# A twelve-stage latent transformer on one core: set-ups reordered, and variances of the third cross-attention taken in pairs

## The chip, the cores and the metric

The kernel runs on 1 core of one Trainium2 chip. The metric is the device time of one execution in microseconds (us); the number quoted for a kernel is the median of its runs. The engines are PE (TensorE), DVE (VectorE), ACT (ScalarE), POOL (GpSimd) and SP (SyncE, which here only issues DMAs). Each runs its own instructions in order and they meet at semaphores.

## The reference

A latent x of 64 rows by 256 is carried through twelve layers, four rounds of cross-attention, self-attention and feed-forward, each added to x. The context has 6272 rows by 256. The layers that matter here:

- layer 1, self-attention, 16 heads; layer 2, a mixture of experts with a shared one: silu(gate) times up, down, routed experts by a softmax over 8;
- layer 3, cross-attention with queries, keys and values rounded to 127 steps per head; the value rows of the whole context are rounded ahead of it;
- layer 6, the third cross-attention, in 8 groups of heads:

```python
qx = _ln(_fp8_linear_pertensor(ln_out, wqx, ...).reshape(b, s, g, hpg, d), qxln_w, qxln_b)
kvx = jnp.einsum('bsi,oi->bso', cond, w_kv_x)
kx, vx = jnp.split(kvx, 2, axis=-1)
kx = _ln(kx.reshape(b, sc, g, d), kxln_w, kxln_b)
xout = _gqa(qx, kx, vx.reshape(b, sc, g, d)).reshape(b, s, nh * d)
```

Every key of every group is normalised over its own 128 elements, so each of the 8 x 6272 keys needs a variance; a small self-attention (q, k, v over the 64 rows) is joined to it and both are projected;
- layer 10, self-attention with a long convolution, done as a Fourier transform by matrix products; layer 11, a mixture of experts with biases.

## The kernel before

Each layer is a stage with a function for each engine; a stage's set-up is a short serial chain (norm, transposes, projection), and `busy(pe, n, bank)` (L523 to L528) puts n bf16 products on constants into such gaps of PE. Weights come through a ring of four slots in the order of `PIECES`, each load on SP waiting until so many pieces have been used; `x2_kx`, which is wanted last, is loaded first of x2's and keeps its slot longest.

**Values for x1.** DVE rounds 49 tiles of context values (`quantise`, L1706) in pieces of six tiles, two buffers, which ACT narrows to int8 (`narrow_values`, L1714). Pieces 3 and 4 stand in stage 1 before the self-attention, 5 behind it, 6 to 8 in stage 2 (f0) before silu (L892); L917 adds f0's output to x. In x1, DVE scales and rounds the queries (L1935, L1940), PE transposes them, DVE spreads them over a tile (L1947), and the scores follow (L1874).

**x2 (stage 6).** Six weight blocks give queries, keys and values of the 64 rows (`block`, L2132), with turns, heads and normalisation on the other engines. Then come steps: `step(scored, weighed, ahead)` scores group `scored` while it weighs the values of group `weighed`. The first step scores group 0 alone, six steps score group g and weigh g - 1, the seventh as well but with no group ahead, and the last only weighs. The context is cut into 13 chunks (NC), twelve of 512 rows and one of 128. For chunk c PE does, in this order:

```python
for c in range(NC):
    if weighed is not None:
        weigh(weighed, c)                 # L2215, 8 products of 257 columns
    if scored is not None:
        if c + 3 < NC:
            keys(scored, c + 3)           # L2109, 4 products of 512
        if c + 1 < NC:
            variance(scored, c + 1)       # L2188, L2189, 16 of one column
            scores(scored, c + 1)         # L2205, 8 of 128
```

ACT copies the keys (L2597) and squares them (L2604); `low_half` (L2397, DVE) makes the low bf16 half of the squares, which with the high half is averaged by the products of `variance`. `read_var` (L2408, DVE) adds the epsilon, POOL raises to -1/2 (L2733), `scale` (L2420, DVE) multiplies the scores with it, writing over the chunk of S that has just been weighed, `running_max` (L2432) keeps a maximum over chunks. DVE's order in step c is scale(c), read_var(c+1), running_max(c), shift(c+2) of the weighed group (L2455, then exp on ACT, L2665), low_half(c+2). At the group's end `top_of_lanes` (L2438) reduces the maximum over four lanes; PE issues keys 0 and 1 of the group ahead, and then `turn_top` (L2222) transposes it.

**f3 (stage 11)** starts with nine products for the experts' biases (L1327), then the norm (L542) and its transposes (L577); a3 (stage 10) has two places with `busy(pe, 3, 7)` in its middle.

Of the kernel before, what the change touches and what calls it, by code (L numbers as in the profile page):

```python
# [23 lines left out]
T = 64  # L24
D = 256
# [93 lines left out]
def for_query_groups(w):  # L119
# [22 lines left out]
    + [(6, "x2_kx", 2048), (6, "x2_qx0", 2048), (6, "x2_qx1", 2048), (6, "x2_q0", 2048), (6, "x2_q1", 2048), (6, "x2_k", 2048),  # L142
       (6, "x2_v", 2048), (6, "x2_vx", 2048)]
# [198 lines left out]
def perceiver(nc, io, first=0, last=11):  # L342
# [8 lines left out]
    released = [n for _, n, _ in pieces]  # L351
    if "x2_kx" in released:
        released.remove("x2_kx")
        released.insert(released.index("x2_vx"), "x2_kx")
    slot_of, nth_in_slot, release_before = [], [], []
    for n in range(len(pieces)):
        if n < NSLOT:
            slot_of.append(n)
            nth_in_slot.append(1)
            release_before.append(0)  # L360
        else:
            old = piece_no[released[n - NSLOT]]
            slot_of.append(slot_of[old])
            nth_in_slot.append(nth_in_slot[old] + 1)
            release_before.append(n - NSLOT + 1)
# [5 lines left out]
    with ExitStack() as stack:  # L371
        def sb(name, shape, dt=F32):
# [15 lines left out]
            "rounded": (("x1_q_ready", 3, 1), ("x2_in_ready", 6, 2), ("x2_cat_ready", 6, 3)),  # L388
# [10 lines left out]
            "tile_ready": (("x1_tile_ready", 3, 1), ("x2_tile_ready", 6, 2 * GROUPS)),  # L399
# [96 lines left out]
        def W(name):  # L496
            n = piece_no[name]
            if n in late:
                a = sum(pieces[i][2] for i in late[:late.index(n)])
                return keysT[:, :, :].rearrange("p k n -> p (k n)")[:, a:a + pieces[n][2]]  # L500
            return ring[:, slot_of[n], 0:pieces[n][2]]

        def weights_here(eng, name):
# [5 lines left out]
            eng.wait_ge(sem(f"weights_in{slot_of[n]}"), 16 * nth_in_slot[n])  # L509
# [47 lines left out]
        def norm_pool(pool, n):  # L557
            k = norm_no[n]
            if k == 0:
# [5 lines left out]
                     10: (4, 1), 11: (3, 5)}  # L565
# [222 lines left out]
        def self_attention(s, bias):  # L788
# [4 lines left out]
            def dve_(dve):  # L793
                norm_vector(dve, s)
                if s == 1:
                    quantise(dve, 3, 4)
                mha_vector(dve, s)
                if s == 1:
                    quantise(dve, 5)
                residual_vector(dve, s, bank(6, D, T), (sem("projected"), outs.index(s) + 1))  # L800

            def act_(act):
                norm_scalar(act, s)
                if s == 1:
                    narrow_values(act, 3, 4)
                mha_scalar(act, s)
                if s == 1:
                    narrow_values(act, 5)
# [49 lines left out]
        def f0_tensor(pe):  # L858
# [17 lines left out]
            busy(pe, 6, 6)  # L876
# [4 lines left out]
            pe.transpose(ps[:, 3, 0:T], f0_small, C("ident")[0:T, 0:T]).then_inc(sem("f0_hT_psum"), 1)  # L881
            pe.wait_ge(sem("f0_hT"), since("f0_hT", 1))
# [12 lines left out]
        def f0_vector(dve):  # L895
            norm_vector(dve, 2)
            quantise(dve, 6, 7, 8)
# [16 lines left out]
            link(dve, "dve", dve.tensor_reduce(f0_weight, f0_exp, AX, ALU.add))  # L914
            dve.wait_ge(sem("f0_out_psum"), since("f0_out_psum", 1))
# [4 lines left out]
        def f0_scalar(act):  # L920
            norm_scalar(act, 2)
            act.wait_ge(sem("f0_part_psum"), 1)
            act.activation(f0_act, bank(0), ACT.Tanh, scale=0.5).then_inc(sem("f0_tanh"), 1)
            act.wait_ge(sem("f0_hidden_psum"), since("f0_hidden_psum", 1))
            act.activation(f0_small, ps[0:T, 4, 0:128], ACT.Tanh, scale=0.5).then_inc(sem("f0_tanh"), 1)
            narrow_values(act, 6, 7, 8)
# [94 lines left out]
        def f1_vector(dve):  # L1021
# [24 lines left out]
            for n in range(4):  # L1046
# [3 lines left out]
                dve.scalar_tensor_tensor(act, act, f1_pair_gates[:, n:n + 1], u, ALU.mult, ALU.mult).then_inc(sem("f1_hidden"), 1)  # L1050
            dve.wait_ge(sem("f1_lows_psum"), since("f1_lows_psum", 1))
# [4 lines left out]
            if runs(6):  # L1056
                weights_here(dve, "x2_kx")
                x2_key_weights(dve, 0)
# [145 lines left out]
        def a3_tensor(pe):  # L1204
# [22 lines left out]
            busy(pe, 3, 7)  # L1227
# [9 lines left out]
            busy(pe, 3, 7)  # L1237
# [82 lines left out]

        def f3_tensor(pe):
# [1731 lines left out]
```

## Time and profile before

| | |
|---|---|
| runs | 1062.67, 1064.81, 1066.28 us; median 1064.81 |
| profiled execution | 1061.59 us, span 1059.8 us |
| mean granted clock of TensorE | 0.99 of full speed |
| busy share of the span | PE 94%, DVE 68%, ACT 34%, POOL 15% |
| instructions | PE 7822, DVE 1909, ACT 627, POOL 143 |

The profiled execution is the one whose instructions are shown; its time is larger than its span by what lies before the first and behind the last instruction. Busy time is a share of the whole span, over stages with different limits: it doesn't say which engine the others wait for in a given stage. In the timeline a bracket [0.97 <-DMA ...] is the idle time before the instruction and what ended it; instructions without one had no idle time that the trace shows. The two levels of TensorE's clock are 1.2 and 2.4 GHz, shown as 0.50 and 1.00.

### The profile page before, as it was taken

Reading aid. Unit: us, or ns where it says so; the run is one execution under the profiler, and the core shown is the slowest. Engines: PE = TensorE matmul, PEld = TensorE weight load, DVE = VectorE, ACT = ScalarE, POOL = GpSimd, SP = SyncE. Lnnn points to the kernel's source line nnn. Section 1 sums busy time; section 2 is a strip of 40 time slices with the busy share of each in tenths; the row PEclk is TensorE's granted clock in tenths of the full one; section 3 lists DMA queues with packets and bytes.
Section 4 is the critical chain, followed back from the end, with each engine's and each line's share of the span. In section 5 each row is a group of like instructions: output and inputs, shape, how many; then the busy total and the mean of one; then the engine's idle time right before and its main releaser. Section 6 shows DMA issues by size and latency. Waiting matters only on the chain.

```text
span 1059.8 us, 20606 instructions
## 1 busy us (share of the span) xinstructions
PE 994.1 (94%) x7822; PEld 657.2 (62%) x7846; DVE 716.2 (68%) x1909; ACT 358.4 (34%) x627; POOL 156.9 (15%) x143
## 2 busy tenths in 40 slices
PE   6999999998789988899999999999999999988898
PEld 4776677675335544365777777677777777743455
DVE  3777767768779834787676767767676767743343
ACT  2332333334428721443333333333343332301211
POOL 0000000001000010233222323222222323000000
PEclk9999999999999999998999999999999999899999
DMA  7100101002229996860000000000000000232430
GB/s 284 41 22 22 38 20 40 20 5 96 99 62 188 192 313 217 320 241 2 1 1 1 1 0 0 0 0 0 0 0 0 0 1 2 79 140 88 174 159 4
DMA packets 68729, 76.09 MB, mean 72 GB/s; under 512 B 52544, under 2 KB 59456, under 8 KB 64832
## 3 DMA queue, kind: packets, MB, share of 16 engines
q1 hardware_dynamic: 68240, 74.71, 23.1%
q8 instruction: 36, 0.59, 0.2%
q10 hardware_dynamic: 432, 0.62, 0.2%
q14 instruction: 21, 0.17, 0.0%
HBM read 62.41 MB, written 0.07 MB: 59 GB/s over the span
## 4 chain that ended last, share of the span: by engine, by line
PE 73%; DVE 11%; issue 5%; DMA 4%; ACT 3%; POOL 3%; SPq 0%; DVEq 0%; POOLq 0%; PEldq 0%
PE ps L2215 15%; PE ps L2109 13%; PE ps L1480 8%; PE ps L2205 7%; PE ps L1470 4%; PE ps L1491 4%; PE ps L1514 2%; PE ps L1526 2%; POOL x_sum L2733 2%; ACT vals L2016 2%; DMA x_keys<-vals 2%; DVE S L2420 1%; PE ps L528 1%; PE ps L1874 1%; PE ps L2817 1%
## 5 line engine op out<-in xcount | busy, mean ns | idle before, releaser
L2215 PE MATMUL ps<-vals,S 128*128 128x257 f32 x784 | 188.5, 384 | 0.7 <-ACT S L2665 0.7
L2109 PE MATMUL ps<-keysT,row_biases_sb 128*128 128x512 f32 (+1 forms) x416 | 186.3, 573 | 1.0 <-DVE row_biases_sb L2094 0.9
L2733 POOL TENSOR_TENSOR x_sum<-x_max,consts 128x4 f32<-128x4 f32 (+1 forms) x104 | 133.6, 1285 | 322.4 <-DVE x_max L2408 322.4
L2420 DVE SCALAR_TENSOR_TENSOR S<-ps,x_sum,keysT 128x128 f32<-128x128 f32 x392 | 110.9, 344 | 73.3 <-PE ps L2215 64.2
L2215 PEld LDWEIGHTS ps<-vals,S 128*128 128x128 f32 x784 | 143.3, 192 | 19.0 <-issue 1.0
L2665 ACT ACTIVATE S<-S 128x512 f32<-128x512 f32 (+1 forms) x104 | 62.7, 606 | 219.1 <-DVE S L2455 218.5
L2205 PE MATMUL ps<-x_q,x_keys 128*128 128x128 f32 x784 | 114.2, 288 | 0.0
L2109 PEld LDWEIGHTS ps<-keysT,row_biases_sb 128*128 128x128 f32 x416 | 76.6, 192 | 57.7 <-issue 52.6
L2205 PEld LDWEIGHTS ps<-x_q,x_keys 128*128 128x128 f32 x784 | 96.4, 193 | 0.0
L1480 PE MATMUL ps<-ring,S 128*128 128x512 f32 x196 | 92.2, 593 | 0.5 <-DVE ps L1621 0.5
L2597 ACT COPY x_keys<-ps 128x512 f32<-128x512 f32 (+1 forms) x104 | 57.1, 549 | 67.5 <-PE ps L2109 34.3
L1594 ACT ACTIVATE S<-ps 128x2048 f32<-128x2048 f32 (+1 forms) x25 | 46.1, 1843 | 82.3 <-PE ps L1526 76.1
L528 PE MATMUL ps<-consts 128*128 128x512 bf16 x253 | 65.7, 380 | 3.7 <-issue 0.5
L2397 DVE TENSOR_TENSOR sw_key_out<-wide 128x512 bf16<-128x512 f32 (+1 forms) x104 | 67.7, 652 | 0.7 <-ACT wide L2604 0.7
L2455 DVE TENSOR_TENSOR S<-S,xnT 128x512 f32<-128x512 f32 (+1 forms) x104 | 66.7, 654 | 0.3
L2432 DVE TENSOR_TENSOR wide<-wide,S 128x512 f32<-128x512 f32 x96 | 63.3, 659 | 0.3
L2604 ACT ACTIVATE wide<-ps 128x512 f32<-128x512 f32 (+1 forms) x104 | 60.0, 577 | 0.0
L1642 DVE TENSOR_SCALAR S<-ps,mask_sb 128x256 f32<-128x256 f32 x49 | 23.7, 484 | 52.6 <-PE ps L1480 31.1
L1470 PE MATMUL ps<-S,ring 128*128 128x256 f32 (+1 forms) x200 | 50.8, 398 | 8.9 <-DMA S<-ctxT 8.2
L1480 PEld LDWEIGHTS ps<-ring,S 128*128 128x128 f32 x196 | 35.3, 190 | 25.9 <-issue 24.7
L562 POOL TENSOR_TENSOR rstd<-var_eps,consts 64x1 f32<-64x1 f32 x13 | 7.1, 550 | 296.4 <-DVE var_eps L548 260.0
L2408 DVE TENSOR_SCALAR x_max<-ps 128x4 f32<-128x4 f32 (+1 forms) x104 | 16.5, 159 | 48.4 <-PE ps L2189 48.3
(453 smaller groups left out, 1366.1 us busy)
## 6 DMA issues: line engine op xcount, KB each, us to landing
ring<-weights SPq DMA_DIRECT2D x24, 1024.0 KB, 5.9
keysT<-ctxT SPq DMA_DIRECT2D x2, 3136.0 KB, 14.9
vals<-ctxN SPq DMA_DIRECT2D x1, 6272.0 KB, 24.3
S<-ctxT SPq DMA_DIRECT2D x12, 512.0 KB, 4.1
ring<-weights SPq DMA_DIRECT2D x6, 768.0 KB, 7.1
keysT<-weights SPq DMA_DIRECT2D x1, 1792.0 KB, 8.8
keysT<-weights SPq DMA_DIRECT2D x1, 1536.0 KB, 12.0
row_biases_sb<-row_biases SPq DMA_DIRECT2D x1, 1416.0 KB, 12.0
```

Of the source, the lines that this page charges most:

```text
L528: pe.matmul(ps[:, b, :], product[:, 0:128], moving, start=True, stop=True)
L1470: ins = pe.matmul(ps[:, sw_keys_bank, TWO * o:TWO * o + n * TILE], w[:, 256 * k + 128 * o:256 * k + 128 * o + 128], sw_ctxT[ph][:, k, TWO ...
L1480: ins = pe.matmul(bank(sw_vk_bank), sw_ctxT[ph][:, k, a:a + TILE], w[:, 512 + 768 * k:1024 + 768 * k], start=k == 0, stop=k == KT - 1)
L2109: ins = pe.matmul(ps[:, x2_key_bank(g, c), 0:width(c)], x2_wk[:, k, :], ctxT[:, k, span(c)], start=k == 0, stop=k == KT - 1)
L2205: ins = pe.matmul(ps[:, 3 + c % 2, 128 * s:128 * s + 128], x2_keys[:, c % 2, TILE * s:TILE * s + TILE], x2_q[:, :], start=True, stop=True)
L2215: ins = pe.matmul(bank(6, D + 1), S[:, a:a + TILE], ctx_and_ones[:, SUB * c + s, :], start=c == 0 and s == 0, stop=c == NC - 1 and s == su ...
L2397: dve.tensor_tensor(x2_low[c % 2][:, 0:width(c)], x2_dev[:, c % 2, 0:width(c)], high_half(c), ALU.subtract)\
L2420: ins = dve.scalar_tensor_tensor(S[:, a:a + TILE], ps[:, 3 + c % 2, 128 * s:128 * s + 128], x2_inv[:, c % 2, s:s + 1], x2_tile_const, ALU. ...
L2432: ins = dve.tensor_tensor(best, best, S[:, span(c)], ALU.max)
L2455: dve.tensor_tensor(chunk, chunk, spread(x2_top, 1, subs(c)), ALU.subtract).then_inc(sem("x2_shifted"), 1)
L2665: act.activation(chunk, chunk, ACT.Exp, scale=SCALE2).then_inc(sem("x2_exp"), 1)
L2733: pool.tensor_tensor(x2_inv[:, c % 2, 0:n], x2_var[:, c % 2, 0:n], C("neg_half").broadcast_to([128, n]), ALU.pow)\
```

## The change

Set-ups. In stage 1 one piece of values is rounded before the attention and one after it, and in f0 three before silu and one behind the router; the last tile is a piece of its own. x1's scaling by 0.25 is joined to the addition of the bias, POOL scales the bias in stage 2, and rounding, transposes and tile go in two halves. x2's first key weights come by a DMA of their own into `x2_wk`; `x2_kx` moves to the end of x2's pieces, and four loads wait on x2's blocks rather than on the count of used pieces. In x2's set-up turn 3 stands before keys 2 on PE, the heads on ACT before a normalise, two low halves on DVE before a wait. Six of f3's nine bias products stand in a3's two `busy` places.

The loop. Variances are made for chunks (0), (1, 2), (3, 4) to (11, 12) together, on PE in even steps behind keys(c+3); DVE's low_half(c+2) stands in even steps right behind scale(c), in odd ones last; `read_var` and the power handle up to 8 columns at once, 7 times a group for 13. `top_of_lanes` is replaced: the running maximum is folded to 256 and to 128 columns at c = 11 and joined with the last chunk at c = 12.

```diff
-    + [(6, "x2_kx", 2048), (6, "x2_qx0", 2048), (6, "x2_qx1", 2048), (6, "x2_q0", 2048), (6, "x2_q1", 2048), (6, "x2_k", 2048),
-       (6, "x2_v", 2048), (6, "x2_vx", 2048)]
+    + [(6, "x2_qx0", 2048), (6, "x2_qx1", 2048), (6, "x2_q0", 2048), (6, "x2_q1", 2048), (6, "x2_k", 2048),
+       (6, "x2_v", 2048), (6, "x2_kx", 2048), (6, "x2_vx", 2048)]
...
-                     10: (4, 1), 11: (3, 5)}
+                     10: (4, 1), 11: (4, 5)}
...
-                    quantise(dve, 3, 4)
+                    quantise(dve, 3)
                 mha_vector(dve, s)
                 if s == 1:
-                    quantise(dve, 5)
+                    quantise(dve, 4)
...
-            busy(pe, 6, 6)
+            busy(pe, 2, 6)
...
+            busy(pe, 2, 4)
...
-            quantise(dve, 6, 7, 8)
+            quantise(dve, 5, 6, 7)
...
+            quantise(dve, 8)
...
+            narrow_values(act, 5)
             act.wait_ge(sem("f0_part_psum"), 1)
             act.activation(f0_act, bank(0), ACT.Tanh, scale=0.5).then_inc(sem("f0_tanh"), 1)
+            narrow_values(act, 6)
...
+            narrow_values(act, 7, 8)
+        def f0_pool(pool):
+            norm_pool(pool, 2)
+            if runs(3):
+                pool.tensor_scalar(R("q1"), R("q1"), 0.25, None, ALU.mult)
...
+                dve.wait_ge(sem("x2_first_in"), 16)
+                x2_key_weights(dve, 0)
...
-            busy(pe, 3, 7)
+            f3_biases(pe, F3_BIASES[0])
...
-            busy(pe, 3, 7)
+            f3_biases(pe, F3_BIASES[1])
...
+        F3_BIASES = ((0, 1, 4), (2, 3, 5), (6, 7, 8))
+        def f3_biases(pe, places):
+            weights_here(pe, "f3_up0")
+            b1 = W("f3_up0")[:, 2 * F3_UP_WIDTH + KT * 16 + D:]
+            pe.wait_ge(sem("f3_selected"), since("f3_selected", 1))
+            for m in places:
+                pair = F3_ORDER[m]
+                pe.matmul(f3_bank(m), f3_select[:, 128 * pair:128 * pair + 128], b1, start=m % 2 == 0, stop=False, skip_group_check=True)
...
+            f3_biases(pe, F3_BIASES[2])
...
+        value_parts = [(6 * i, 6 * i + 6) for i in range(7)] + [(48, NT), (42, 48)]
...
-            busy(pe, 6, 3)
+            for i in range(2):
+                pe.wait_ge(sem("x1_q_ready"), since("x1_q_ready", i + 1))
+                for j in range(4):
+                    a = 512 * i + 128 * j
+                    ins = pe.transpose(ps[:, X1_TURNED[i], j * T:(j + 1) * T], x1_q_rows[:, a:a + 128], C("ident")[0:T, 0:T])
+                ins.then_inc(sem("x1_qT_psum"), 1)
+            busy(pe, 3, 3)
...
-            link(dve, "dve", dve.tensor_tensor(x1_q, bank(0, D, T), R("q1"), ALU.add))
-            link(dve, "dve", dve.tensor_scalar(x1_q, x1_q, 0.25, None, ALU.mult))
+            link(dve, "dve", dve.scalar_tensor_tensor(x1_q, bank(0, D, T), 0.25, R("q1"), ALU.mult, ALU.add))
...
-            dve.tensor_scalar(x1_q_rows.rearrange("p (j r d) -> p j r d", j=PAIRS, r=4), spread(cut(x1_q, PAIRS, 32), 2, 4), MAGIC, MAGIC,
-                              ALU.add, ALU.subtract).then_inc(sem("x1_q_ready"), 1)
+            for i in range(2):
+                pairs = slice(4 * i, 4 * i + 4)
+                dve.tensor_scalar(x1_q_rows.rearrange("p (j r d) -> p j r d", j=PAIRS, r=4)[:, pairs], spread(cut(x1_q, PAIRS, 32)[:, pairs], 2, 4),
+                                  MAGIC, MAGIC, ALU.add, ALU.subtract).then_inc(sem("x1_q_ready"), 1)
+            x1_tile_of(dve, 0)
...
-            dve.wait_ge(sem("x1_qT_psum"), 1)
-            dve.tensor_tensor(x1_queries.rearrange("p (j h t) -> p j h t", j=PAIRS, h=2), spread(cut(bank(1), PAIRS, T), 2, 2),
-                              spread(spread(C("two_heads"), 1, PAIRS), 3, T), ALU.mult).then_inc(sem("x1_tile_ready"), 1)
+            x1_tile_of(dve, 1)
...
+        x2_behind_block = {"x2_k": 0, "x2_v": 1, "x2_kx": 2, "x2_vx": 3} if runs(5) and runs(6) else {}
+        X2_TOGETHER = [(0,)] + [(c, c + 1) for c in range(1, NC, 2)]
+        X2_READS = len(X2_TOGETHER)
+        x2_read_of = lambda c: (c + 1) // 2
...
-            def variance(g, c):
-                pe.wait_ge(sem("x2_square_low"), g * NC + (c + 1))
-                if c >= 1 or not (isinstance(g, int) and g == 0):
-                    pe.wait_ge(sem("x2_var_read"), g * NC + c)
-                for s in range(subs(c)):
-                    a = SUB * (c % 2) + s
-                    tile_of = slice(TILE * s, TILE * s + TILE)
-                    pe.matmul(ps[:, 7, a:a + 1], high_half(c)[:, tile_of], x2_mean, start=True, stop=False)
-                    ins = pe.matmul(ps[:, 7, a:a + 1], x2_low[c % 2][:, tile_of], x2_mean, start=False, stop=True)
-                ins.then_inc(sem("x2_keys_var"), 1)
+            def variance(g, r):
+                chunks = X2_TOGETHER[r]
+                pe.wait_ge(sem("x2_square_low"), g * NC + (chunks[-1] + 1))
+                if r >= 1 or not (isinstance(g, int) and g == 0):
+                    pe.wait_ge(sem("x2_var_read"), g * X2_READS + r)
+                for c in chunks:
+                    for s in range(subs(c)):
+                        a = SUB * (c % 2) + s
+                        tile_of = slice(TILE * s, TILE * s + TILE)
+                        pe.matmul(ps[:, 7, a:a + 1], high_half(c)[:, tile_of], x2_mean, start=True, stop=False)
+                        ins = pe.matmul(ps[:, 7, a:a + 1], x2_low[c % 2][:, tile_of], x2_mean, start=False, stop=True)
+                    ins.then_inc(sem("x2_keys_var"), 1)
...
                         if c + 3 < NC:
                             keys(scored, c + 3)
+                        if c % 2 == 0 and c + 2 < NC:
+                            variance(scored, c // 2 + 1)
                         if c + 1 < NC:
-                            variance(scored, c + 1)
                             scores(scored, c + 1)
...
-            def read_var(g, c):
-                dve.wait_ge(sem("x2_keys_var"), g * NC + (c + 1))
-                if c >= 2:
-                    dve.wait_ge(sem("x2_inverse"), g * NC + (c - 1))
-                elif c == 0 and not (isinstance(g, int) and g == 0):
-                    dve.wait_ge(sem("x2_inverse"), g * NC)
-                a, n = SUB * (c % 2), subs(c)
-                dve.tensor_scalar(x2_var[:, c % 2, 0:n], ps[:, 7, a:a + n], LN_EPS, None, ALU.add).then_inc(sem("x2_var_read"), 1)
+            def read_var(g, r):
+                dve.wait_ge(sem("x2_keys_var"), g * NC + (X2_TOGETHER[r][-1] + 1))
+                if r >= 1 or not (isinstance(g, int) and g == 0):
+                    dve.wait_ge(sem("x2_inverse"), g * X2_READS + r)
+                n = SUB if r == 0 else 2 * SUB
+                dve.tensor_scalar(x2_max[:, 0:n], ps[:, 7, 0:n], LN_EPS, None, ALU.add).then_inc(sem("x2_var_read"), 1)
...
+                if c == NC - 1:
+                    dve.wait_ge(sem("x2_running"), g * X2_RUNS + X2_RUNS)
+                    dve.tensor_tensor(x2_lanes_top, x2_running[:, 0:128], S[:, span(c)], ALU.max).then_inc(sem("x2_max"), 1)
+                    return
...
-            def top_of_lanes(g):
-                dve.wait_ge(sem("x2_running"), g * NC + NC)
-                dve.tensor_reduce(x2_lanes_top, x2_running.rearrange("p (s r) -> p r s", s=SUB), AX, ALU.max).then_inc(sem("x2_max"), 1)
+            def fold_running(g):
+                for i, n in enumerate((256, 128)):
+                    dve.wait_ge(sem("x2_running"), g * X2_RUNS + (NC - 1 + i))
+                    best = x2_running[:, 0:n]
+                    dve.tensor_tensor(best, best, x2_running[:, n:2 * n], ALU.max).then_inc(sem("x2_running"), 1)
...
                         scale(scored, c, weighed)
-                    if scored is not None and c + 1 < NC:
-                        read_var(scored, c + 1)
+                    if scored is not None and c % 2 == 0 and c + 2 < NC:
+                        low_half(scored, c + 2)
                     if scored is not None:
                         running_max(scored, c)
+                    if scored is not None and c == NC - 2:
+                        fold_running(scored)
                     if weighed is not None and c >= 1 and c + 2 < NC:
                         shift(weighed, c + 2)
-                    if scored is not None and c + 2 < NC:
+                    if scored is not None and c % 2 == 0 and c + 2 < NC:
+                        read_var(scored, c // 2 + 1)
+                    if scored is not None and c % 2 == 1 and c + 2 < NC:
                         low_half(scored, c + 2)
...
+            def inverse(g, r):
+                pool.wait_ge(sem("x2_var_read"), g * X2_READS + (r + 1))
+                if r >= 1 or not (isinstance(g, int) and g == 0):
+                    pool.wait_ge(sem("x2_scores"), since("x2_scores", g * NC + X2_TOGETHER[r][0]))
+                n = SUB if r == 0 else 2 * SUB
+                pool.tensor_tensor(x2_sum[:, 0:n], x2_max[:, 0:n], C("neg_half").broadcast_to([128, n]), ALU.pow)\
                     .then_inc(sem("x2_inverse"), 1)
...
+                if name == "f1_experts3" and runs(6):
+                    first = piece_from["x2_kx"]
+                    sp.dma_start(x2_wk, cut(io["weights"][:, first:first + KT * 1024], KT, 1024)[:, :, 0:GD]).then_inc(sem("x2_first_in"), 16)
...
+                if pieces[n][1] in x2_behind_block:
+                    sp.wait_ge(sem("x2_block_psum"), x2_behind_block[pieces[n][1]] + 1)
+                else:
+                    sp.wait_ge(weights_used, n - NSLOT + 1)
```

## Rows read from the trace of the kernel before

**Rows 1.** Windows: stretch, us; busy PE, PEld, DVE, ACT, POOL; clock, DMA, GB/s.

```profile
431.60:439.00 7.40, 4.86 (x24) 1.48 (x20) 6.22 (x35) 1.81 (x5) 3.08 (x3) 1.00 0.88 302
...
483.40:490.20 6.80, 6.53 (x22) 3.88 (x20) 6.07 (x19) 0.00 (x0) 2.44 (x2) 0.50 0.00 0
...
609.08:667.66 58.58, 58.28 (x355) 42.46 (x355) 41.68 (x115) 20.76 (x42) 16.61 (x13) 1.00 0.00 0
...
903.20:910.00 6.80, 6.29 (x19) 4.71 (x19) 5.41 (x12) 3.79 (x8) 0.00 (x0) 0.50 0.37 117
```

**Rows 2.** Timeline, PE, an even chunk: start, us, engine, line.

```profile
642.78 1.88 PE L2109 MATMUL ps<-keysT,row_biases_sb 128*128 128x512 f32 x4
...
644.50 0.17 PE L2188 MATMUL ps<-sw_value_part,wide 128*128 128x1 bf16 x1
...
644.70 1.14 PE L2205 MATMUL ps<-x_q,x_keys 128*128 128x128 f32 x8
```

**Rows 3.** Timeline, DVE, the same chunk.

```profile
642.98 1.13 DVE L2420 SCALAR_TENSOR_TENSOR S<-ps,x_sum,keysT 128x128 f32<-128x128 f32 x4 [0.77 <-PE ps L2215]
...
646.17 0.68 DVE L2397 TENSOR_TENSOR sw_key_out<-wide 128x512 bf16<-128x512 f32 x1
```

**Rows 4.** Timeline, PE, the end of a group.

```profile
660.05 0.17 PE L2188 MATMUL ps<-sw_value_part,wide 128*128 128x1 bf16 x1
...
663.77 3.60 PE L2109 MATMUL ps<-keysT,row_biases_sb 128*128 128x512 f32 x8
...
667.66 0.33 PE L2222 MATMUL ps<-consts,attendedT 128*128 128x128 f32 x1 [0.30 <-DVE attendedT L2438]
```

**Rows 5.** Timeline, DVE, the same end.

```profile
660.25 1.13 DVE L2420 SCALAR_TENSOR_TENSOR S<-ps,x_sum,keysT 128x128 f32<-128x128 f32 x4 [0.31 <-PE ps L2215]
...
661.30 0.15 DVE L2408 TENSOR_SCALAR x_max<-ps 128x4 f32<-128x4 f32 x1
...
662.23 0.28 DVE L2397 TENSOR_TENSOR sw_key_out<-wide 128x128 bf16<-128x128 f32 x1
...
666.58 1.03 DVE L2438 TENSOR_REDUCE attendedT<-wide 128x128 f32<-128x512 f32 x1
```

**Rows 6.** Instructions of one line, POOL's power: shortest, median, longest in ns.

```profile
L2733 POOL TENSOR_TENSOR x_sum<-x_max,consts x104: 911/1317/1447, 449.6 to 899.1; 128x4 f32<-128x4 f32 x96, 128x1 f32<-128x1 f32 x8
```

**Rows 7.** Timeline, PE, the first step of x2.

```profile
483.17 0.18 PE L2188 MATMUL ps<-sw_value_part,wide 128*128 128x1 bf16 x1 [1.47 <-DVE sw_key_out L2397]
```

**Rows 8.** Timeline, stage 1.

```profile
263.85 3.96 DVE L1706 TENSOR_TENSOR wide<-vals,S 128x1536 int16<-128x1536 f32 x2
...
264.65 1.94 PE L673 MATMUL ps<-ring,xnT 128*64 128x512 f32 x8 [0.45 <-ACT xnT L582]
...
267.73 0.68 DVE L727 TENSOR_TENSOR S<-ps,row_biases_sb 128x512 f32<-128x512 f32 x1
```

**Rows 9.** Timeline, stage 2.

```profile
287.60 0.43 DVE L1706 TENSOR_TENSOR wide<-vals,S 128x256 int16<-128x256 f32 x1 [3.51 <-ACT vals L1714]
...
293.42 0.87 DVE L917 TENSOR_TENSOR x_sb<-x_sb,ps 64x256 f32<-64x256 f32 x2 [0.70 <-PE ps L886]
```

**Rows 10.** Timeline, stage 3.

```profile
299.08 0.28 DVE L1935 TENSOR_SCALAR sw_key_out<-sw_key_out 64x256 f32<-64x256 f32 x1
...
303.61 1.98 PE L1874 MATMUL ps<-keysT,x_probsT 32*128 32x512 f32 x10
```

**Rows 11.** Timeline, set-up of x2.

```profile
436.13 1.94 PE L2132 MATMUL ps<-ring,S 128*64 128x512 f32 x8 [2.19 <-DMA ring<-weights]
```

**Rows 12.** DMA issues of one window, SP: first and last issue, and the landing.

```profile
L2936 SPq DMA_DIRECT2D ring<-weights x1: 328/328/328, 420.5 to 420.5; - x1
...
DMA to landing us min/median/max: 9.6/9.6/9.6
```

**Rows 13.** Timeline, stages 10 and 11.

```profile
1038.43 0.41 DVE L542 TENSOR_SCALAR xn<-x_sb,moments,rstd 64x256 f32<-64x256 f32 x1 [0.66 <-POOL rstd L562]
...
1040.29 0.33 PE L577 MATMUL ps<-consts,xn 64*128 64x64 f32 x2
```

More of the change, by code:

```diff
@@ L350, in perceiver @@
     piece_no = {n: k for k, (_, n, _) in enumerate(pieces)}
[L351 to L365, printed above, removed]
     piece_from, at = {}, 0
@@ L500, in W @@
                 return keysT[:, :, :].rearrange("p k n -> p (k n)")[:, a:a + pieces[n][2]]
-            return ring[:, slot_of[n], 0:pieces[n][2]]
+            return ring[:, n % NSLOT, 0:pieces[n][2]]
         def weights_here(eng, name):
@@ L1323, in f3_tensor @@
             w = W("f3_up0")[:, 2 * F3_UP_WIDTH:]
-            b2, b1 = w[0:NE, KT * 16:KT * 16 + D], w[:, KT * 16 + D:KT * 16 + D + FF]
-            pe.wait_ge(sem("f3_selected"), since("f3_selected", 1))
-            for m, pair in enumerate(F3_ORDER):
-                pe.matmul(f3_bank(m), f3_select[:, 128 * pair:128 * pair + 128], b1, start=m % 2 == 0, stop=False, skip_group_check=True)
+            b2 = w[0:NE, KT * 16:KT * 16 + D]
+            f3_biases(pe, F3_BIASES[2])
             norm_tensor(pe, 11)
@@ L1711, in narrow_values @@
             for part in parts:
-                a, b = 6 * part, min(6 * part + 6, NT)
+                a, b = value_parts[part]
                 act.wait_ge(sem("values_rounded"), part + 1)
@@ L1928, in x1_tensor, with x1_tile_of @@
             out_tensor(pe, 3, attended, w[:, 512:1024], "x1")
+        def x1_tile_of(dve, i):
+            dve.wait_ge(sem("x1_qT_psum"), i + 1)
+            out = x1_queries[:, 512 * i:512 * i + 512].rearrange("p (j h t) -> p j h t", j=4, h=2)
+            dve.tensor_tensor(out, spread(cut(ps[:, X1_TURNED[i], 0:4 * T], 4, T), 2, 2), spread(spread(C("two_heads"), 1, 4), 3, T), ALU.mult)\
+               .then_inc(sem("x1_tile_ready"), 1)
         def x1_vector(dve):
@@ L2088, in x2_key_weights @@
                 dve.wait_ge(sem("x2_keys_psum"), before * NC + NC)
-            of_group = cut(W("x2_kx"), KT, 1024)[:, :, ds(g * GD, GD)]
+            of_group = x2_wk if isinstance(g, int) and g == 0 else cut(W("x2_kx"), KT, 1024)[:, :, ds(g * GD, GD)]
             dve.tensor_reduce(x2_wk_mean, of_group, AX, ALU.add).then_inc(sem("x2_wk_sum"), 1)
@@ L2705, in x2_scalar @@
             take_heads(0)
+            normalise(2)
             take_heads(1)
-            normalise(2)
             copy_const(0)
+            take_heads(2)
             copy_const(1)
-            take_heads(2)
             take_values()
@@ L2739, in x2_pool @@
                     .then_inc(sem("x2_block_inverse"), 1)
-            for c in range(NC):
-                inverse(0, c)
+            for r in range(X2_READS):
+                inverse(0, r)
             with pool.Fori(1, GROUPS) as g:
-                for c in range(NC):
-                    inverse(g, c)
+                for r in range(X2_READS):
+                    inverse(g, r)
         STAGES[6] = (x2_tensor, x2_vector, x2_scalar, x2_pool)
```

53 lines of the change are left out of this document (19 added, 34 removed).

## The prediction

> **What bounds the kernel now.** The profiled execution has a span of 1059.8 us and took 1061.59 us, so 1.8 us lie around the span. By the page's first part PE is busy in 94% of it, VectorE (DVE) in 68%, GpSimd (POOL) in 15%: a faster DVE or POOL pays only where PE waits for it. Then I read the windows, stage by stage: one group step of the third cross-attention (x2) lasts 58.58 us, with PE busy 58.28 of them at clock 1.00 and DVE busy 41.68 [rows 1]. Seven such steps fill 410 us. There the change touches what PE never waits for, so the question is whether the new order makes it wait. The timeline of a chunk [rows 2, 3] and of a group's end [rows 4, 5] answers that; the set-ups are read from their own waits [rows 8 to 13].
>
> **Set-ups and ends, part by part.**
>
> *a1's first piece (stage 1).* The product that L727 reads ends at 264.65 + 1.94 = 266.59, but L727 starts at 267.73, with no wait of its own: two quantise instructions (3.96 us together, from 263.85) stand in front [rows 8]. With one of them behind the attention L727 starts about 0.09 after the product, as after any product: gain 267.73 − 266.68 = 1.05. The piece that moved lies beside the attention's last products on PE, for which DVE has nothing else; uncovered it would cost its 1.98.
>
> *f0 (stage 2).* The last small quantise waited 3.51 us for ScalarE's (ACT) narrowing and stood ahead of silu; it goes [rows 9]. Then the other end limits: the big quantise moved behind the router (1.75 us, the second half of a 1.98-us one without its narrow) stands before L917, which was at 293.42 and can be at about 291.7. Gain 1.7. If the quantise were hidden, PE's order would allow 2.45. The removed dummy products are only as long as the wait they filled.
>
> *x1 (stage 3).* One multiply goes (0.28 busy, 0.32 with its link; the scaling of q1 moves to POOL, which could cost no more than one power-sized instruction, 0.9, if it were not), and rounding, transposes and tile run in halves, so the scores, at 303.61 [rows 10], start when PE has turned the second half. I take 1.25; bounds 0.3 (the multiply alone) and 2.0 (half of rounding and of the 1.22-us tile too).
>
> *x2's set-up.* PE waited 2.19 us at 436.13 for weights [rows 11]. In the new order that block reads the piece one place earlier in the queue. The piece in that place was issued at 420.5 and landed 9.6 us later, at 430.1 [rows 12]: the wait goes. Of the DVE wait before the key weights 0.7 comes off ahead of it. Three turns, heads and normalise steps are reordered around waits of 0.9 each, of which PE's other work hides nearly all, and 0.4 is lost again. Gain 2.5; bounds 1.5 and 3.5. SP now waits on x2's blocks for four pieces: nothing stands behind them on SP's queue before x2_proj0, which is wanted over 400 us later.
>
> *a3 and f3 (stages 10, 11).* Six of the nine bias products replace dummies and leave f3's head. x normalised is ready at 1038.43 + 0.41 = 1038.84, its transposes start at 1040.29 [rows 13]: 1.45 are to be had, I take 1.3 because the real products end 0.1 later in a3 than dummies.
>
> Sum of these: 1.05 + 1.7 + 1.25 + 2.5 + 1.3 = 7.8 us off.
>
> **The loop: an even chunk.** Before, low_half of chunk c+2 was DVE's last work in step c, and PE used it one step later. Now the variance of a pair (c+1, c+2) stands on PE right behind keys(c+3), and needs low_half(c+2), which DVE makes in the same step behind scale(c). Scale(c) cannot be earlier: it overwrites the chunk that PE has just weighed, and starts 0.20 after keys(c+3), at 642.98 against 642.78 [rows 2, 3]. From there it holds DVE for 1.05 (660.25 to the next operation at 661.30) [rows 5], low_half takes 0.68 [rows 3], and the variance's load and product start 0.11 behind. So 0.20 + 1.05 + 0.68 + 0.11 = 2.04 us after keys(c+3) starts, while PE is free for it at 644.50 − 642.78 = 1.72 [rows 2]: a stall of 0.32, at c = 0, 2, 4, 6, 8: 1.6 us a group. In return six of thirteen sets of short products no longer stand between keys and scores; the number of products is the same, and what a set costs beside them is 0.07 (0.20 from 644.50 to 644.70, eight starts 0.025 apart). Gain 6 × 0.07 = 0.42. Even chunks together +1.2.
>
> **The loop: a group's end.** At c = 10 no keys stand between weighing and variance. PE would be ready at 660.05 [rows 4]; low_half(12), formerly at 662.23 and used later, takes 0.28 − 0.03 behind scale(10), which starts at 660.25 [rows 5]. 661.30 + 0.28 + 0.11 = 661.69: a stall of 1.64. The set of variances gone from the next step gives 0.12 back, so keys 0 and 1 of the group ahead, at 663.77 before, start 1.52 later, at 665.29. They stand 3.43 ahead of what follows (3.60 with their pipelined end [rows 4]), so L2222 comes at 668.72 instead of 667.66: of the 1.52 its old wait on DVE, 667.66 − 663.77 − 3.43 = 0.46, takes up the rest. DVE, with the 1.03-us reduction [rows 5] replaced by two folds (256 and 128 columns, 0.41 and 0.28 by size) inside chunk 11, is ready at 668.12, before PE. So +1.05. Six groups at 1.2 + 1.05 = 2.25 make 13.5. In the last group no keys fill the end and L2222 waits on DVE's chain: 1.2 + 0.45 = 1.65. Loop: +15.1.
>
> POOL now does 7 powers of up to 8 columns for 13 of 4. One of 1 column takes 0.91, the usual one about 1.32 [rows 6]: 0.137 a column, so 1.86; bounds 1.32 (size costs nothing) and 2.6 (two of 4). In the group steps it lies beside weighing: read 3.4 us after keys start, it lets scale(c+1) begin at 5.5 (6.2 at 2.6) where 4.9 + 0.2 would do; the odd chunk has only 3.0 us of DVE work in 4.6, so PE sees none of it. The Trainium skill's page "GPSIMD Engine Reference", section "3.1 Elementwise — side-by-side cycle accounting", counts some 2.6 cycles an element for a tensor_tensor; four more columns would be next to nothing, the power some 1.33, and step 0 below would cost about 3 instead of 4. The rows of 1 and 4 columns speak for the larger value.
>
> **Step 0, where only scores run.** Here DVE and POOL are the chain at the end: PE waits 1.47 for low_half at 483.17, and then runs at clock 0.50 from 483.40 to 490.20 [rows 7, 1]. In pairs the cycle is: variance 0.58, read 0.25, power 1.86, scale 1.14, running maximum and low_half 1.3, scale 1.05, low_half 0.68, 0.11 = 6.9 us, where PE needs 5.8. Five pairs put the last variance at 488.1 (4.9 later), with PE idle 3.8 ahead of it. Behind it one power serves both last chunks and the end is 6.5 instead of 8.3 us, so L2222 comes 2.7 later. The longer idle starts the slow clock sooner, 1.3 more. I take +4; bounds 0 (power 1.32 and clock as before) and +8 (power 2.6, a second stretch at half clock).
>
> **Sum.** 1061.59 − 7.8 + 15.1 + 4 = 1072.9 for the profiled execution. It lies 3.2 below the median of the runs, 1064.81; the forecast is put beside that median: 1064.81 + 11.3 = 1076.1.
>
> **The rivals.**
> *A, faster: the pair's wait is covered.* If DVE gets low_half out within 1.72 us of keys' start (scale shorter than 1.05, or started before the weighing ends), the even chunks gain 0.42, and the end gains 0.5 by the fold: 7 × 0.94 = 6.6 off. With the set-ups 1064.81 − 7.8 − 6.6 = 1050.4. It decides at 1.72 us. Against it: all 0.20, 1.05 and 0.68 are rows with no slack between.
> *B, much slower: the stall at each group's end drops the clock.* 903.20 to 910.00, behind the last group's wait, ran at 0.50, as did 483.40 to 490.20 [rows 1]. 6.8 us at half clock cost some 3.4; over 7 groups up to 24, at least 12 if half of them fall: 1088 to 1100. Against: the 2.19-us wait at 433.9 to 436.1 left 431.60 to 439.00 at 1.00 [rows 1], and the new one is 1.64. The page "TensorE: Matmul & The Clock Gate", Part 1, of the Trainium skill says the clock follows how busy the engine has lately been; by that rule a single short wait in a loop 99% busy leaves it, which the row at 436 bears out.
> *C, little change: the stalls are half of mine.* PE's queue hides part of them, or scores wait anyway; the loop costs 4 to 8, the set-ups give 7.8: 1061 to 1068.
>
> **Chances.** The stalls as worked out 0.64; A 0.16; B 0.08; C 0.12. The forecast's own range is 1068 to 1086 (set-ups 5 to 10 off, loop 11 to 20, step 0 0 to 8). To leave out no more than 2 in 10 the range must take in C, the corner of A next to it and that of B: 1058 to 1090. About 3.2 us, 0.3%, is what tells from no change: faster 0.16 + 0.03 of C, same 0.07 of C and the forecast's edge, slower the rest, 0.74.
>
> **What would show it.** In the group steps: a wait of about 0.3 at each even variance and 1.6 at the last, both put down to DVE's low_half, a step of 60.8 us, no wait at L2222; in step 0 POOL instructions of 1.8 and PE idle before the last variance. Set-ups: no DMA wait at x2's second query block, L727, L917 and L577 each one to two microseconds sooner after their stage's start. I am wrong if group steps are 58.6 or less (A), or show 0.50 in each (B).

## The result, and the profile after

The changed kernel took 1074.62 us (median of four runs, 1067.77 to 1074.80) against 1063.74 before (1062.65 to 1066.28): ratio 1.0083, interval 1.0045 to 1.0121: slower by 0.8%. The profile shown is of the run of 1067.77 us, span 1066.0, with a granted clock of 0.995; the other three and a fifth run of 1072.80 had 0.990. Before had 0.990 in its profile too. That matters for what is compared below: the steps of the loop run at clock 1.00 in both profiles and can be compared directly, the spans cannot.

The windows of 60.9 us of one group step, and of the stretch behind the idle time in x2's first step (columns as in rows 1):

```profile
477.40:484.30 6.90, 6.36 (x25) 4.25 (x26) 5.46 (x19) 0.14 (x1) 1.63 (x1) 0.51 0.00 0
...
608.00:668.90 60.90, 58.52 (x356) 42.07 (x355) 40.49 (x109) 20.75 (x41) 11.10 (x7) 1.00 0.00 0
```

PE is busy 58.5 us, as before [rows 1] to 0.2; the step, from one `turn_top` to the next, is 60.96 us and so 2.37 longer, and DVE and POOL do less. What is added is idle time of PE. PE's waits on two lines, by what ended them (total us, times, longest):

```profile
PE ps L2212 <- DVE sw_key_out L2422: 23.4, 47, 3.4
PE ps L2246 <- DVE attendedT L2452: 2.8, 1, 2.8
```

L2212 is the variance's first product (L2188 before), L2422 is `low_half`, L2246 is `turn_top`, which waited in seven of the eight groups before and now waits in the last alone. The timeline of an even chunk, to be put beside [rows 2, 3]:

```profile
642.39 1.88 PE L2131 MATMUL ps<-keysT,row_biases_sb 128*128 128x512 f32 x4
642.60 1.13 DVE L2443 SCALAR_TENSOR_TENSOR S<-ps,x_sum,keysT 128x128 f32<-128x128 f32 x4 [1.21 <-PE ps L2239]
643.64 0.68 DVE L2422 TENSOR_TENSOR sw_key_out<-wide 128x512 bf16<-128x512 f32 x1
...
644.45 0.18 PE L2212 MATMUL ps<-sw_value_part,wide 128*128 128x1 bf16 x1 [0.18 <-DVE sw_key_out L2422]
...
644.87 1.14 PE L2229 MATMUL ps<-x_q,x_keys 128*128 128x128 f32 x8
```

The variance starts 2.06 after the keys; 1.72 was free. The bracket says 0.18 rather than 0.34, because the shown end of the matmul before it lies behind the point where the next could have started: starts are what to subtract. At a group's end, beside [rows 4, 5]:

```profile
658.45 1.90 PE L2239 MATMUL ps<-vals,S 128*128 128x257 f32 x8
661.85 0.17 PE L2212 MATMUL ps<-sw_value_part,wide 128*128 128x1 bf16 x1 [1.50 <-DVE sw_key_out L2422]
665.49 3.60 PE L2131 MATMUL ps<-keysT,row_biases_sb 128*128 128x512 f32 x8
668.92 0.27 PE L2246 MATMUL ps<-consts,attendedT 128*128 128x128 f32 x1
```

```profile
660.40 1.13 DVE L2443 SCALAR_TENSOR_TENSOR S<-ps,x_sum,keysT 128x128 f32<-128x128 f32 x4
661.44 0.28 DVE L2422 TENSOR_TENSOR sw_key_out<-wide 128x128 bf16<-128x128 f32 x1
```

POOL's power (median 1.63 us for 8 columns, beside rows 6), and the waits of x2's first step, beside rows 7:

```profile
L2763 POOL TENSOR_TENSOR x_sum<-x_max,consts x56: 1007/1633/1636, 439.1 to 906.9; 128x8 f32<-128x8 f32 x48, 128x4 f32<-128x4 f32 x8
```

```profile
471.62 0.18 PE L2212 MATMUL ps<-sw_value_part,wide 128*128 128x1 bf16 x1 [0.84 <-DVE sw_key_out L2422]
477.94 0.19 PE L2212 MATMUL ps<-sw_value_part,wide 128*128 128x1 bf16 x1 [3.43 <-DVE sw_key_out L2422]
```

The set-ups: L727 of before is now L712, and waits for PE; L917 is L904; the scores of x1, the second query block of x2 and f3's transposes follow [rows 8 to 13]:

```profile
266.09 0.69 DVE L712 TENSOR_TENSOR S<-ps,row_biases_sb 128x512 f32<-128x512 f32 x1 [1.02 <-PE ps L658]
...
290.14 0.86 DVE L904 TENSOR_TENSOR x_sb<-x_sb,ps 64x256 f32<-64x256 f32 x2
```

```profile
299.16 1.99 PE L1883 MATMUL ps<-keysT,x_probsT 32*128 32x512 f32 x12
...
425.50 3.17 PE L2154 MATMUL ps<-ring,S 128*64 128x512 f32 x14
...
1046.49 0.34 PE L562 MATMUL ps<-consts,xn 64*128 64x64 f32 x2
```

L2154, the blocks, has no wait on a DMA. Read from stage to stage by the norms' first instruction, the set-ups gained 1.1 (a1), 1.7 (f0), 1.6 (x1), 2.4 (end of f1 and x2's set-up, without a stretch at clock 0.50 that the profile before had at 408.3 to 411.7, worth 1.7) and 1.4 (f3): 8.2 together. The loop then lost 2.9 in the first step and 16.7 in seven groups. The border between x2's set-up and its first step is POOL's last power of the set-up here (442.73 before, 433.78 now). With PE's first variance as the border (448.96 before, 438.53 now) the set-up gained 3.9 and the first step lost 4.4; together they are +0.5 either way.

### The profile page after: what moved, and what is told of

The parts are those of the page before. It is cut to its first block, busy times and chain, and to the rows that moved or that the text cites. A ratio compares the mean times of both kernels' runs of the same rounds, so it can differ in the third digit from the quotient of the medians.

```text
span 1066.0 us, 20340 instructions
## 1 busy us (share of the span) xinstructions
PE 988.4 (93%) x7812; PEld 651.2 (61%) x7836; DVE 706.9 (66%) x1870; ACT 358.2 (34%) x627; POOL 112.7 (11%) x96
## 4 chain that ended last, share of the span: by engine, by line
PE 68%; DVE 18%; issue 6%; ACT 3%; DMA 3%; POOL 1%; DVEq 0%; SPq 0%; ACTq 0%; POOLq 0%
PE ps L2239 14%; PE ps L2131 9%; PE ps L1483 8%; PE ps L2229 7%; DVE S L2443 5%; PE ps L1473 4%; PE ps L1494 4%; DVE sw_key_out L2422 3%; PE ps L1517 2%; PE ps L1529 2%; ACT vals L2031 2%; DMA x_keys<-vals 2%; PE ps L2212 2%; PE ps L513 1%; PE ps L1883 1%
## 5 line engine op out<-in xcount | busy, mean ns | idle before, releaser
L2763 POOL TENSOR_TENSOR x_sum<-x_max,consts 128x8 f32<-128x8 f32 (+1 forms) x56 | 88.5, 1580 | 385.3 <-DVE x_max L2431 385.3
L2229 PE MATMUL ps<-x_q,x_keys 128*128 128x128 f32 x784 | 109.9, 283 | 0.0
L2229 PEld LDWEIGHTS ps<-x_q,x_keys 128*128 128x128 f32 x784 | 99.5, 193 | 15.8 <-issue 15.3
L2422 DVE TENSOR_TENSOR sw_key_out<-wide 128x512 bf16<-128x512 f32 (+1 forms) x104 | 67.7, 652 | 1.4 <-ACT wide L2636 1.4
L513 PE MATMUL ps<-consts 128*128 128x512 bf16 x243 | 63.4, 380 | 3.6 <-PE ps L2277 0.4
L2459 DVE TENSOR_TENSOR wide<-wide,S 128x512 f32<-128x512 f32 x88 | 60.6, 689 | 4.3
L2212 PEld LDWEIGHTS ps<-sw_value_part,wide 128*128 128x128 bf16 x392 | 22.5, 97 | 59.0 <-issue 34.5
L2212 PE MATMUL ps<-sw_value_part,wide 128*128 128x1 bf16 x392 | 26.6, 165 | 23.4 <-DVE sw_key_out L2422 23.4
```

Source lines behind the costliest of these rows:

```text
L513: pe.matmul(ps[:, b, :], product[:, 0:128], moving, start=True, stop=True)
L2212: pe.matmul(ps[:, 7, a:a + 1], high_half(c)[:, tile_of], x2_mean, start=True, stop=False)
L2229: ins = pe.matmul(ps[:, 3 + c % 2, 128 * s:128 * s + 128], x2_keys[:, c % 2, TILE * s:TILE * s + TILE], x2_q[:, :], start=True, stop=True)
L2422: dve.tensor_tensor(x2_low[c % 2][:, 0:width(c)], x2_dev[:, c % 2, 0:width(c)], high_half(c), ALU.subtract)\
L2763: pool.tensor_tensor(x2_sum[:, 0:n], x2_max[:, 0:n], C("neg_half").broadcast_to([128, n]), ALU.pow)\
```

## The experiments

Group steps are the distance between two `turn_top`, median of six; times are medians of 4 to 12 runs, of one run where it says so, with the interval of the ratio to the kernel before, which ran beside them at 1062.7 to 1064.1.

| kernel | group step | time | ratio |
|---|---|---|---|
| before | 58.59 | 1063.7 | |
| changed | 60.96 | 1074.6 | 1.0045 to 1.0121 |
| e1 set-ups only | 58.59 | 1048.8 | 0.9849 to 0.9901 |
| e2 loop only | 60.94 | 1083.6 | 1.0164 to 1.0220 |
| e3 low half first, all | 59.79 | 1063.0 | 0.9978 to 1.0021 |
| e4 low half first, last only | 60.87 | 1069.2 | 1.0037 to 1.0081 |
| e5 last pair apart | 60.53 | 1070.3 | 1.0034 to 1.0077 |
| e6 apart and low half first | 59.42 | 1059.0 | 0.9938 to 0.9974 |
| e8 set-ups and fold | 58.12 | 1047.5 | 0.9820 to 0.9877 |
| e9 old order of weights | 60.96 | 1077.9, one run | |
| e10 e6 with an early read | 58.51 | 1053.4 | 0.9865 to 0.9929 |
| e11 power twice | 65.14 | 1106.9, one run | |

**The two halves apart.** e1 has the loop of before (`variance(g, c)`, `low_half` last, `top_of_lanes`) and all set-up edits; e2 the reverse.

> The changed kernel with the whole loop of x2 as it was before (variances one by one, low halves last, reduction at the group's end); all set-up edits stay. My theory: the time is the sum of two independent parts, set-ups about -7.8 to -9, loop about +17 to +19. So 1063.7 - 8 = about 1056, group step 58.6 us, and every stage outside the loop as in the changed kernel. Rival: set-up gains don't add up (some are only jitter of the clock and the first DMA); then 1060 to 1064.

> The kernel before with the loop's part alone: pairs, fold, new order of the low halves. My theory: group step 60.95 us against 58.59, over seven steps about +16, the first step some +3 to +4: 1063.7 + 19 = about 1083. Rival: the loop's cost comes partly from how x2 is entered (the set-ups shift the first step against the clock); then under 1078.

e2 came out as expected. The loop behaves as one part: 60.94 with the old set-ups, 58.59 with the old loop. The window of one step of e1 is that of rows 1:

```profile
540.00:598.58 58.58, 58.28 (x355) 42.48 (x355) 41.67 (x115) 20.80 (x42) 16.51 (x13) 1.00 0.01 1
```

But e1 gained 13.9 us, not 8, and there my expectation of 1056 failed. In its profile the clock stood at 0.50 for 10.2 us (294, 891) and for a short stretch at the very end, in that of before for 20.4 (408, 483, 903, 988). 10.2 us less of half clock are worth at most 5.1 us (at most, because x2's first step, from its first variance, took 41.80 us at 1.00 in e1 and 42.94 before, with 6.8 us of it at 0.50: 1.1 apart and not 3.4); with 8.2 of set-ups and 0.5 of an earlier start of the first norm that is 13.8 of the 13.95 between the two profiled executions. The runs agree: span times mean granted clock is 1041.9 us in the mean of e1's runs against 1050.7 in those of before, 8.9 less, which is what the set-ups gave, and the rest is clock. Five of e1's six runs had 0.995, where the 19 of before beside them had 0.990 in the mean. Why e1 ran with fewer slow stretches is open. Shorter idle time in the set-ups alone doesn't do it: e3, e4, e5, e6, e8 and e10 have the same set-up edits, and their runs had 0.988 to 0.992 in the mean. Which stretch falls differs; x2's first step kept 1.00 in e1's profile and not in e8's, which has the same order there but for the fold.

**Mending the stall.** e3 moves one instruction, e4 does so at c = 10 alone:

```diff
+                    if scored is not None and c % 2 == 0 and c + 2 < NC:
+                        low_half(scored, c + 2)
                     if scored is not None:
                         scale(scored, c, weighed)
-                    if scored is not None and c % 2 == 0 and c + 2 < NC:
-                        low_half(scored, c + 2)
```

> The changed kernel with one edit: in even chunks low_half(c+2) stands on DVE before scale(c) rather than behind it. My theory: the stall is the 1.05 us of scale(c) that stands between the end of weighing and the low half, and nothing else in the pairs costs PE. Then no wait of PE on the low half is left in the group steps, a group takes 58.59 - 0.08 x 6 - 0.4 = about 57.8 to 58.2 us, and the time falls from 1074.6 to about 1052 (1049 to 1056). Rival 1: pairs themselves cost (power of 8 columns, one bank for both): the step stays above 60. Rival 2: the square on ScalarE comes too late, so DVE now waits for it in front of scale(c): step 59 to 60.

> As e3, but only at c = 10, the pair (11, 12); the five other even chunks keep their order. My theory: of 2.38 us a group the end makes about 1.05 and the five even chunks 1.3. So the step goes from 60.95 to about 59.5 (the end's wait on DVE of 0.46 is gone as well through the fold), the time to about 1064. Rival: the end's stall is covered in part by the keys of the group ahead and costs under 0.5 a group: step 60.5, time 1071.

The stall in the even chunks was scale(c) standing in front: in e3 the variance starts 1.72 after the keys again in each of them, PE's waits on `low_half` fall from 47 to 12, and the step falls by 1.17. But the step came out at 59.79 and not at 57.8 to 58.2: my theory missed, and the second rival's range held, with DVE waiting 44 times for ACT's square (41.9 us in all). What is left lies at the group's end:

```profile
655.02 1.91 PE L2239 MATMUL ps<-vals,S 128*128 128x257 f32 x8
658.53 0.17 PE L2212 MATMUL ps<-sw_value_part,wide 128*128 128x1 bf16 x1 [1.61 <-DVE sw_key_out L2422]
```

With 1.74 for the weighing that is a stall of 1.77, no shorter than the 1.65 of the changed kernel. e4, which mends the end alone, missed too: it gained 0.09. Its rows there:

```profile
663.86 0.29 DVE L2422 TENSOR_TENSOR sw_key_out<-wide 128x128 bf16<-128x128 f32 x1 [0.43 <-ACT wide L2638]
664.12 1.13 DVE L2443 SCALAR_TENSOR_TENSOR S<-ps,x_sum,keysT 128x128 f32<-128x128 f32 x4
...
668.25 1.13 DVE L2443 SCALAR_TENSOR_TENSOR S<-ps,x_sum,keysT 128x128 f32<-128x128 f32 x4 [0.92 <-POOL x_sum L2765]
```

```profile
664.29 0.17 PE L2212 MATMUL ps<-sw_value_part,wide 128*128 128x1 bf16 x1 [0.95 <-DVE sw_key_out L2422]
...
671.76 0.33 PE L2246 MATMUL ps<-consts,attendedT 128*128 128x128 f32 x1 [0.25 <-DVE attendedT L2452]
```

The low half now waits for the square of chunk 12, which ACT makes behind an exp and a copy; PE still waits 0.95 (1.12 by starts, 0.53 less than before the edit); and scale(11) then waits for the power of the pair and makes `turn_top` late, which takes 0.41 of it back. So two more limits stood close behind the first: ACT's square and POOL's power.

**Taking the last pair apart.** The first line of the edit in both; what makes, reads and raises the two single variances follows it. e6 has the low half first as well:

```diff
-        X2_TOGETHER = [(0,)] + [(c, c + 1) for c in range(1, NC, 2)]
+        X2_TOGETHER = [(0,)] + [(c, c + 1) for c in range(1, NC - 2, 2)] + [(NC - 2,), (NC - 1,)]
```

> The changed kernel with the last pair taken apart: variances of chunks 11 and 12 one by one, low_half(12) last in step 10, as before; the five other pairs stay with their order. My theory: the end of a group costs because chunk 11 must wait for the low half of chunk 12 and then for a power that serves both. Taken apart, that is gone: step 58.59 + 1.3 (five even chunks at 0.34 less 0.07) - 0.4 (fold) = about 59.5 us against 60.96, time about 1065 to 1067. Rival: the end's loss lies in the fold and the last chunk's maximum, not in the pair; then the step stays above 60.5.

> Both mendings: last pair apart, and low_half(c+2) before scale(c) in the four other even chunks that have one and in the first. My theory: no wait of PE on a low half is left, and five sets of short products fewer at 0.07 each: step about 57.8 to 58.2 us, against 58.59 before; time about 1046 (1043 to 1050), a few us under the kernel with the set-ups alone. Rival: moving scale behind the low half delays the powers and the end, which eats the saving; step 58.6 or more, time 1049 or more.

Both missed by a microsecond or more and came out on their rivals' side, e5 just so. In e5 the five even chunks keep their stalls of 0.34, the variance of chunk 11 stalls 0.51, and `turn_top` waits again, now for a scale(12) that waits 0.83 for its own power. In e6 the wait had moved to chunk 11:

```profile
653.66 1.13 DVE L2447 SCALAR_TENSOR_TENSOR S<-ps,x_sum,keysT 128x128 f32<-128x128 f32 x4 [1.92 <-POOL x_sum L2769]
...
656.12 0.69 DVE L2426 TENSOR_TENSOR sw_key_out<-wide 128x512 bf16<-128x512 f32 x1
```

```profile
656.93 0.17 PE L2214 MATMUL ps<-sw_value_part,wide 128*128 128x1 bf16 x1 [0.99 <-DVE sw_key_out L2426]
...
664.66 0.33 PE L2248 MATMUL ps<-consts,attendedT 128*128 128x128 f32 x1 [0.41 <-DVE attendedT L2456]
```

The power for chunks 9 and 10 holds scale(9), then shift and low_half(11) follow, and at c = 9 the keys are only 128 columns wide, so there is no slack. e10 reads the variance right behind scale(c):

```diff
                         scale(scored, c, weighed)
+                    if scored is not None and c % 2 == 0 and c + 2 < NC:
+                        read_var(scored, c // 2 + 1)
```

> e6 with one edit more: in even chunks the read of the pair's variance stands right behind scale(c), ahead of the running maximum and the shift. In e6 the wait had moved: POOL's power for chunks 9 and 10 started at 651.90 and held scale(9) until 653.66, 0.8 us later than weighing allowed, so low_half(11) came 0.99 late at the group's end, where keys are short. My theory: this chain over POOL is what is left of the pairs' cost. Read 1.2 us sooner, it lets scale(9) start when weighing ends; the wait of 0.99 falls below 0.3 and L2248's 0.41 goes: step 59.42 to 58.1 to 58.6, time from 1059 to about 1051. Rival: low_half(11) is late by DVE's own work in the short ninth chunk, whatever POOL does; step stays above 59.

```profile
652.83 1.13 DVE L2447 SCALAR_TENSOR_TENSOR S<-ps,x_sum,keysT 128x128 f32<-128x128 f32 x4 [1.34 <-PE ps L2241]
```

```profile
656.11 0.17 PE L2214 MATMUL ps<-sw_value_part,wide 128*128 128x1 bf16 x1 [0.24 <-DVE sw_key_out L2426]
```

Scale(9) waits for weighing again, and the step is 58.51, in the range expected. The chain over POOL was most of what e6 had left. Two waits remain, both at the end: 0.24 at chunk 11, under 0.3 as expected, and 0.26 at L2248, which I had expected to go. Counted in starts they are 0.40 and 0.42; less the five times 0.08 that the pairs save (below) this is, to a few hundredths, the distance to e8's 58.12.

**POOL doubled.** Each power is done twice:

> The changed kernel with POOL's power done twice, one after the other (each 1.63 us for 8 columns). My theory: in most chunks the power lies beside weighing with slack, but not at the group's end nor in the first step of x2: group step +0.5 to +1.5 (61.5 to 62.5), first step +7 to +10. Rival: the power is the chain of every pair: +1.6 six times a group, steps near 70, 70 us in all. Other rival: it is nowhere on the path, steps stay at 60.96.

The group step grew by 4.18, far over the 0.5 to 1.5 that I expected and under half of the rival's 9.6; the even chunks' stalls grew as well, to 0.6. The first step grew by 8.1 from its first variance, inside the expected 7 to 10. It is a single run, at a mean clock of 0.978, so the steps count and not the time. PE's wait at the group's end is 2.92 here, and behind it the clock falls in six of the seven groups (3.4 us at 0.51, worth 1.7 of the 4.18), which it does in none of the changed kernel's with 1.50. Between the two lies e3: its wait at the end shows 1.62 in five groups, and behind one of them (599.2 to 602.6) the clock was at 0.50, which made that step 61.06 for 59.79. The rows of e11:

```profile
682.91 0.17 PE L2212 MATMUL ps<-sw_value_part,wide 128*128 128x1 bf16 x1 [2.92 <-DVE sw_key_out L2422]
```

```profile
684.40:687.70 3.30, 3.30 (x10) 2.58 (x9) 0.26 (x1) 0.00 (x0) 2.70 (x2) 0.51 0.00 0
690.00:745.00 55.00, 53.02 (x322) 37.92 (x320) 33.59 (x90) 19.48 (x37) 18.76 (x12) 1.00 0.00 0
```

**The fold alone.** The set-ups and, of the loop, only `fold_running` and the last maximum:

> The set-ups' edits and of the loop only the folded running maximum; variances one by one in the old order. My theory: L2222 waited 0.46 us at each group's end for DVE, and the fold takes the reduction (1.03 us) off that end: step 58.59 - 0.46 = 58.13, seven times 3.2 off, 1048.8 to about 1045.6. Rival: the fold's extra instructions at chunk 11 delay scale(12) by as much as is saved; step 58.5 or more, no change of time.

The step is 58.12, where the wait of rows 4, in starts, had said 58.13. The time fell by 1.3 and not 3.2: e8's profile had 20.4 us at half clock where e1's had 10.2, ahead of the end, which is up to 5.1 us. It is the fastest kernel of the study, 1.5% under the one before, though its interval overlaps that of e1; the step, not the time, shows the fold's gain.

**The order of the weights.** `x2_kx` is wanted first as well as last: before, DVE read the first group's key weights out of it at the end of f1, which is why it was loaded first, and later groups read theirs in the loop. The small DMA into `x2_wk` is what lets it move behind the others. e9 is the changed kernel with `x2_kx` first again:

> The changed kernel with the old order of x2's weight pieces (x2_kx first, waits on used pieces, first key weights from the ring). My theory: PE waits again some 2.2 us for weights at x2's second query block, and the end of f1 is 0.4 to 2 later: the set-up of x2 ends 2.4 to 4 later against the profile of the changed kernel; the loop's steps stay at 60.96. Rival: the DMA wait is only moved on to another block, and the order is worth under 0.5.

```profile
PE ps L2169 <- DMA ring<-weights: 2.3, 1, 2.3
```

The wait is back, 2.3 us. From f1's norm to POOL's last power of x2's set-up it took 6.6 longer than the changed kernel, but two stretches at clock 0.50 (422.7 and 436.3, 3.4 us each) hold half of that; 3.2 are the order's own, inside the 2.4 to 4 expected, by one profile.

## Why the prediction was right

The forecast was 1076, measured 1074.6; its sign held, and its range, which was wide (1058 to 1090), did too. What carried it is the mechanism: a stall of PE at each pair's variance, put down to `low_half` behind scale, which e3 takes away in the even chunks by moving that one instruction.

- *Even chunks.* 2.04 us from keys to variance forecast, 2.06 measured; every term of the sum stood in the rows (0.21, 1.04, 0.68, 0.13).
- *The group's end.* Wait 1.64 forecast; 661.85 against the 660.20 at which weighing 10 leaves PE free is 1.65. `turn_top` came 7.07 behind it where 7.03 was reckoned. Step +2.37 against +2.25. The last of the seven steps, without keys of a group ahead, grew by 2.22 where 1.65 was reckoned, so the seven make +16.7 and not +15.1.
- *The first step.* +4 forecast; +2.9 measured from POOL's last power, +4.4 from PE's first variance. Set-up and first step together are +0.5 where +1.5 was forecast. Two terms were mis-sized. One is the power: 1.86 taken, 1.63 measured. The Trainium skill's count in "GPSIMD Engine Reference", section "3.1 Elementwise — side-by-side cycle accounting", had given 1.33 by my use of it; the trace lies between, 0.08 a column from 4 to 8. PE idle ahead of the last variance was 3.43 where I had 3.8. The other is the 1.3 for a sooner slow clock: the stretch at half clock lasted 6.8 to 6.9 us, as before, so that term came to nothing. The sum itself doesn't come out of its terms either: they make 6.97 a pair and not 6.9, five times the 1.1 over PE's 5.8 are 5.5 and not 4.9, and 4.9 less the 1.8 from 8.3 to 6.5 is 3.1 and not 2.7. That +4 lay near is partly luck.
- *Set-ups.* 7.8 forecast, 8.2 measured: a1 1.1 (1.05), f0 1.7 (1.7), x1 1.6 (1.25), x2 2.4 (2.5), f3 1.4 (1.3). x1 gave more because its end, too, came 0.4 sooner.
- *What I had not reckoned* is how much the stretches at half clock differ from run to run and from kernel to kernel. In the profiled run 10.2 us ran at 0.50 against 20.4 before, outside the last microseconds, worth up to 5.1 us; the sum without it, 8.2 + 0.5 off and 19.6 on, makes 10.9 against the 11.3 forecast. The three slower runs of the median, at 0.990, gave it back, so the median came out near the sum. Within the sum the loop cost 1.6 more than reckoned, the first step 1.1 less, the set-ups gave 0.4 more, and 0.5 came off ahead of the first norm: that the median agreed to 1.5 us is partly luck.
- *Rivals.* A decides at 1.72 us and 2.06 is over it: fell. B (clock falls at each group's end) did not happen at waits of 1.50, and does at 2.92 in six of seven groups (e11), and once in five at 1.62 (e3): the mechanism is real and the margin was small. The Trainium skill's sentence in "TensorE: Matmul & The Clock Gate", Part 1, that the clock follows how busy the engine has lately been, fits these. C fell with the steps.

What the loop's edits are worth one by one: the fold −0.47 a group, the pairs with all three mendings about +0.39 (58.51 − 58.12), the unmended order another 2.4. Whether some order exists in which pairs beat single variances was not tried; their whole saving is five times 0.08 us a group: eight products of scores take 0.97 behind variances (644.87 to the weighing at 645.84) and 0.89 where none stand ahead (649.30 to 650.19).

## What to carry to other kernels

Batching small operations makes the first result wait for the last input: before pairing, write down when each input is made on the other engines and subtract from when the consumer is free, in starts, not busy time. When a wait is removed and little is gained, look for the next limit within a few tenths of a microsecond, and check the shortest iteration of the loop, where cover is thinnest. Measure a loop edit by its step, since the clock's slow stretches move whole runs by more than such an edit does.

## What the hardware showed unexpectedly

- The same program ran at 1067.8 or at 1072.8 to 1074.8 us, with mean clocks of 0.995 and 0.990.
- A wait of 1.5 us in a loop that is otherwise full left the clock at 1.00 in every group (the changed kernel, e2, e9); one of 1.6 was followed by 3.4 us at half clock in one group of five (e3), one of 2.8 to 2.9 by at least 3.4 us in six of seven (e11).
- POOL's power took 1.01 to 1.12 us for 4 columns at times and 1.3 to 1.45 at others, 1.63 for 8 in the changed kernel, and 1.64 to 2.07 for the same 8 in e10, where it starts earlier; why is open.
